# Two query heads in a pair of neighbouring PSUM banks, each half read by one pass of 1024 columns, with four banks for all other products

## The reference

```
x = x + tanh(g_xattn) * attention(layernorm(x), ctx, ctx, mask)     # 16 heads of 64
x = x + tanh(g_ffn)   * experts(layernorm(x))                       # 8 experts, top 2
attention: q = x Wq^T, k = ctx Wk^T, v = ctx Wv^T by heads
           softmax(q k^T + mask) v, then Wo
experts:   logits = x Wg + bg; p = softmax; the two largest, divided by their sum
           sum over the two of weight * (relu(x W1 + b1) W2 + b2)
```

## Time and profile before

| | |
|---|---|
| runs | 1152.84, 1154.45, 1154.65 us; median 1154.45 |
| the profiled execution | 1155.27 us, span 1153.5 |
| busy in the span | PE 881.5 us, DVE 939.9, ACT 785.6, POOL 710.6 |
| mean granted TensorE clock | 0.921 |

### The profile page before, as it was taken

The page is one execution under the profiler, slowest core; times in us unless marked ns, Lnnn a source line. Parts: engine busy times, 40 slices in busy tenths (PEclk is TensorE's granted clock), DMA queues, the critical chain, the costliest instruction groups (busy, mean ns, idle before and its releaser), DMA issues.

```text
span 1153.5 us, 33826 instructions
## 1 busy us (share of the span) xinstructions
PE 881.5 (76%) x11840; PEld 674.7 (58%) x11840; DVE 939.9 (81%) x2160; ACT 785.6 (68%) x1627; POOL 710.6 (62%) x701
## 2 busy tenths in 40 slices
PE   6787888798788888877897887878898767555560
PEld 4465665566566766666675656666676556444440
DVE  3888898898989897978888989978798987646633
ACT  3877778777677878786887667766887564444540
POOL 3143455547365666564658787755758787778775
PEclk9998899999999999999999998999998897778975
DMA  8367756555467765453445455554445465477773
GB/s 173 75 172 196 206 146 171 153 159 157 130 172 197 207 179 158 107 131 96 116 116 147 121 161 131 128 129 103 109 122 160 119 172 154 145 202 211 209 205 103
DMA packets 250791, 174.53 MB, mean 151 GB/s; under 512 B 39168, under 2 KB 232192, under 8 KB 250624
## 3 DMA queue, kind: packets, MB, share of 16 engines
q1 hardware_dynamic: 242432, 155.57, 50.9%
q0 software_dynamic: 8192, 16.79, 4.9%
HBM read 75.42 MB, written 63.84 MB: 121 GB/s over the span
## 4 chain that ended last, share of the span: by engine, by line
DVE 24%; issue 13%; PE 13%; POOL 8%; ACT 8%; SPq 3%; DMA 2%; DVEq 0%; POOLq 0%; ACTq 0%
PE bank L90 4%; POOL arena L1033 4%; PE bank L92 3%; PE bank L91 3%; DVE qL L726 3%; POOL hidL L1072 2%; DVE vL L901 2%; DVE row_max L929 2%; DVE otL L955 2%; DVE arena L909 2%; DVE x_back L949 2%; POOL slots L1020 2%; DVE row_sum L917 1%; SPq L1153 1%; ACT qH L545 1%
## 5 line engine op out<-in xcount | busy, mean ns | idle before, releaser
L1078 POOL TENSOR_TENSOR ptL<-pt,ptH 128x512 f16<-128x512 f32 x128 | 148.8, 1162 | 250.9 <-ACT pt L651 250.6
L726 DVE TENSOR_TENSOR qL<-bank,qH 128x512 f16<-128x512 f32 x256 | 173.7, 681 | 51.7 <-ACT qH L545 49.5
L545 ACT ACTIVATE qH<-bank 128x512 f16<-128x512 f32 x256 | 152.9, 599 | 43.8 <-PE bank L92 42.6
L1084 POOL TENSOR_TENSOR prob<-prob,row_inv 128x512 f32<-128x512 f32 x128 | 134.9, 1054 | 52.4 <-DVE row_inv L935 52.3
L1020 POOL DMA_INDIRECT slots<-x2hat,slot x128 | 128.1, 1001 | 31.9 <-issue 29.9
L90 PE MATMUL bank<-ptH,vdH 128*128 128x64 f16 x1024 | 120.4, 202 | 33.6 <-DVE arena L909 23.6
L1033 POOL DMA_INDIRECT arena<-slots,slot x128 | 123.1, 962 | 36.1 <-issue 29.7
L90 PE MATMUL bank<-arena,hidH 128*128 128x128 f16 x396 | 83.6, 240 | 69.6 <-POOL hidL L1072 66.9
L90 PEld LDWEIGHTS bank<-ptH,vdH 128*128 128x128 f16 x1024 | 107.9, 118 | 41.2 <-DVE arena L909 27.6
L1072 POOL TENSOR_TENSOR hidL<-arena,hidH 128x512 f16<-128x512 f32 x99 | 115.7, 1169 | 12.2 <-ACT hidH L595 10.8
L91 PE MATMUL bank<-ptL,vdH 128*128 128x64 f16 x1024 | 120.4, 202 | 0.0
(11 more groups left out here) (158 smaller groups left out, 3399.5 us busy)
## 6 DMA issues: line engine op xcount, KB each, us to landing
arena<-expert_weights SPq DMA_DIRECT2D x99, 321.0 KB, 3.1
slots<-zeros SPq DMA_DIRECT2D x60, 512.0 KB, 3.4
vdH<-vH SPq DMA_DIRECT2D x256, 64.0 KB
vdL<-vL SPq DMA_DIRECT2D x256, 64.0 KB
arena<-slots SPq DMA_DIRECT2D x99, 128.0 KB
slots<-arena SPq DMA_DIRECT2D x99, 128.0 KB
x_raw<-in_x SPq DMA_DIRECT2D x16, 256.0 KB, 4.1
ctx_raw<-in_ctx SPq DMA_DIRECT2D x16, 256.0 KB, 4.6
```

Of the source, the lines that this page charges most:

```text
L545: act.activation(qH[:, g % 2, 2 * j + g2, :, h2, :], bk("Q", g, h)[:, :].rearrange("p (b q) -> p b q", b=GB), ACT.Copy).then_inc(s_q_high, 1)
L726: dve.tensor_tensor(qL[at], bk("Q", g, h)[:, :].rearrange("p (b q) -> p b q", b=GB), qH[at], ALU.subtract).then_inc(s_q_low[h % 2], 1)
L1078: pool.tensor_tensor(ptL[:, b % 2, :], pt[:, b % 2, :], ptH[:, b % 2, :], ALU.subtract).then_inc(s_pt_low, 1)
L1084: pool.tensor_tensor(p, p, row_inv[:, b % NPB, :].unsqueeze(2).to_broadcast([P, JG, S]), ALU.mult).then_inc(s_normal, 1)
```

## The change

The two heads of a step now go into one tensor `head_pair` of two neighbouring banks. PE makes both heads' products one after the other at the start of the step and signals once; ACT copies both in one instruction of 1024 columns, and DVE reads both in one. Before PE writes the next pair it waits for DVE's read of the last. The remaining four banks rotate over all other products, so their owners follow each other in another order. On PE, `route` and `positions` move from the middle of the step to behind the experts' output.

```diff
-        bank = [stack.enter_context(nc.psum_tensor(f"bank{i}", [P, N], F32)) for i in range(NBANK)]
+        bank = [stack.enter_context(nc.psum_tensor(f"bank{i}", [P, N], F32)) for i in range(NBANK - 2)]
+        head_pair = stack.enter_context(nc.psum_tensor("head_pair", [P, 2, N], F32))
...
         def evicted(name):
             kind, *at = name
-            if kind == "Q":
-                g, h = at
-                return [(s_q_high, g * H + h + 1), q_lowered(g, h)]
...
-            def queries(g, h):
-                for freed in take_bank("Q", g, h):
-                    pe.wait_ge(*freed)
-                if h == 0:
+            def queries(g, i):
+                at = g * JG + i
+                if at:
+                    pe.wait_ge(s_q_low, at)
+                if i == 0:
                     pe.wait_ge(s_xT_low, g + 1)
-                if g == 0 and h % 4 == 0:
-                    pe.wait_ge(s_wdve, h // 4 + 1)
-                three_passes(pe, bk("Q", g, h)[:, :], (aH[:, h, :], aL[:, h, :]),
-                             (xtH[:, g % 2, :], xtL[:, g % 2, :])).then_inc(s_q, 1)
+                if g == 0 and i % 2 == 0:
+                    pe.wait_ge(s_wdve, i // 2 + 1)
+                for g2 in range(2):
+                    last = three_passes(pe, head_pair[:, g2, :], (aH[:, 2 * i + g2, :], aL[:, 2 * i + g2, :]),
+                                        (xtH[:, g % 2, :], xtL[:, g % 2, :]))
+                last.then_inc(s_q, 1)
...
                 if i == 0:
-                    pe.wait_ge(*q_lowered(g, H - 2))
-                    pe.wait_ge(*q_lowered(g, H - 1))
+                    pe.wait_ge(s_q_low, JG * (g + 1))
...
                 if within(g + 1, GROUPS):
-                    queries(g + 1, 2 * i)
+                    queries(g + 1, i)
                 if within(s // 2, TILES):
                     values(s // 2, s % 2)
-                if within(g + 1, GROUPS):
-                    queries(g + 1, 2 * i + 1)
-                if i == 0 and within(g - 2, GROUPS):
-                    route(g - 2)
...
-                if i == 2 and within(g - 2, GROUPS):
-                    positions(g - 2)
...
                 if unit_at(s - 2) is not None:
                     expert_out(unit_at(s - 2))
+                if i == 0 and within(g - 2, GROUPS):
+                    route(g - 2)
+                if i == 2 and within(g - 2, GROUPS):
+                    positions(g - 2)
...
-                j, h2, g2 = h // 4, h % 4 // 2, h % 2
-                act.activation(qH[:, g % 2, 2 * j + g2, :, h2, :], bk("Q", g, h)[:, :].rearrange("p (b q) -> p b q", b=GB),
-                               ACT.Copy).then_inc(s_q_high, 1)
+                j, h2 = i // 2, i % 2
+                act.activation(qH[:, g % 2, 2 * j:2 * j + 2, :, h2, :],
+                               head_pair[:, :, :].rearrange("p a (b q) -> p a b q", b=GB), ACT.Copy).then_inc(s_q_high, 1)
...
-                if within(g + 1, GROUPS):
-                    queries_high(g + 1, 2 * i + 1)
...
-                at = (slice(None), g % 2, 2 * j + g2, slice(None), h2, slice(None))
-                dve.tensor_tensor(qL[at], bk("Q", g, h)[:, :].rearrange("p (b q) -> p b q", b=GB), qH[at],
-                                  ALU.subtract).then_inc(s_q_low[h % 2], 1)
+                at = (slice(None), g % 2, slice(2 * j, 2 * j + 2), slice(None), h2, slice(None))
+                dve.tensor_tensor(qL[at], head_pair[:, :, :].rearrange("p a (b q) -> p a b q", b=GB), qH[at],
+                                  ALU.subtract).then_inc(s_q_low, 1)
...
-                if within(g + 1, GROUPS):
-                    queries_low(g + 1, 2 * i + 1)
```

More of the change, by code:

```diff
@@ L243, in flamingo_block @@
         s_xT_low, s_ctxT_low, s_x2T_low = sem("xT_low"), sem("ctxT_low"), sem("x2T_low")
-        s_q_low = [sem(f"q_low{i}") for i in range(2)]
-        s_v_low, s_max, s_shift, s_sum, s_inv, s_o_low, s_res = (
-            sem(n) for n in ("v_low", "max", "shift", "sum", "inverse", "o_low", "residual"))
+        s_q_low, s_v_low, s_max, s_shift, s_sum, s_inv, s_o_low, s_res = (
+            sem(n) for n in ("q_low", "v_low", "max", "shift", "sum", "inverse", "o_low", "residual"))
         s_marked, s_mask_in = sem("score_banks_marked"), sem("mask_in_bank")
@@ L263, in flamingo_block @@
             sem(n) for n in ("pt_low", "normal", "rank_before", "rank_add", "hid_low"))
-        def q_lowered(g, h):
-            return s_q_low[h % 2], g * (H // 2) + h // 2 + 1
         def x_loaded(g):
@@ L537, in _, with queries_high @@
         def _(act):
-            def queries_high(g, h):
-                act.wait_ge(s_q, g * H + h + 1)
-                if h == 0 and g >= 2:
+            def queries_high(g, i):
+                act.wait_ge(s_q, g * JG + i + 1)
+                if i == 0 and g >= 2:
                     act.wait_ge(s_scores, GB * (g - 1))
-                if h == 0 and g == 0:
+                if i == 0 and g == 0:
                     act.wait_ge(s_wdve, H // 4 + 5)
-                j, h2, g2 = h // 4, h % 4 // 2, h % 2
-                act.activation(qH[:, g % 2, 2 * j + g2, :, h2, :], bk("Q", g, h)[:, :].rearrange("p (b q) -> p b q", b=GB),
-                               ACT.Copy).then_inc(s_q_high, 1)
+                j, h2 = i // 2, i % 2
+                act.activation(qH[:, g % 2, 2 * j:2 * j + 2, :, h2, :],
+                               head_pair[:, :, :].rearrange("p a (b q) -> p a b q", b=GB), ACT.Copy).then_inc(s_q_high, 1)
             def transposed_high(name, g, high, after, freed, count):
@@ L624, in _ @@
                 if within(g + 1, GROUPS):
-                    queries_high(g + 1, 2 * i)
+                    queries_high(g + 1, i)
                 if within(s // 2, TILES):
@@ L666, in _ @@
                 if i == 6 and within(g + 2, GROUPS):
-                    transposed_high("xT", g + 2, xtH[:, g % 2, :], s_xT, (s_q, H * (g + 1)) if g >= 0 else None, s_xT_high)
+                    transposed_high("xT", g + 2, xtH[:, g % 2, :], s_xT, (s_q, JG * (g + 1)) if g >= 0 else None, s_xT_high)
                 if i == 6 - sooner and within(g + 1, GROUPS):
@@ L720, in ln_shift, with queries_low @@
                                          ALU.mult).then_inc(s_ln[w]["shift"], 1)
-            def queries_low(g, h):
-                dve.wait_ge(s_q_high, g * H + h + 1)
-                j, h2, g2 = h // 4, h % 4 // 2, h % 2
-                at = (slice(None), g % 2, 2 * j + g2, slice(None), h2, slice(None))
-                dve.tensor_tensor(qL[at], bk("Q", g, h)[:, :].rearrange("p (b q) -> p b q", b=GB), qH[at],
-                                  ALU.subtract).then_inc(s_q_low[h % 2], 1)
+            def queries_low(g, i):
+                dve.wait_ge(s_q_high, g * JG + i + 1)
+                j, h2 = i // 2, i % 2
+                at = (slice(None), g % 2, slice(2 * j, 2 * j + 2), slice(None), h2, slice(None))
+                dve.tensor_tensor(qL[at], head_pair[:, :, :].rearrange("p a (b q) -> p a b q", b=GB), qH[at],
+                                  ALU.subtract).then_inc(s_q_low, 1)
             def transposed_low(name, g, low, high, after, count):
@@ L896, in _ @@
                 if within(g + 1, GROUPS):
-                    queries_low(g + 1, 2 * i)
+                    queries_low(g + 1, i)
                 if within(s // 2, TILES):
```

## The result

| | before | after |
|---|---|---|
| median of 4 runs each | 1153.68 us | 1236.51 us (1235.24 to 1246.74) |
| ratio | | 1.0737, 95% interval 1.0679 to 1.0795 |
| span of the profiled execution | 1153.5 us | 1234.7 us |
| mean granted TensorE clock | 0.921 | 0.910 |

The table counts one run of the kernel before more than the one ahead of the prediction. The change makes the kernel slower by some 83 us (81 between the two spans). The direction, which was given 0.83, is right; 1188 and the range up to 1210 are too low.

What follows compares the result with a forecast made beforehand. DVE was taken as nearest to a bound where the change acts, though often starved waiting for ACT or PE. Groups without experts +9, with experts +23, start and end +1 gave +33 us on 1155.3: 1188 us, range 1160 to 1210.

Steps and rivals of the forecast that it cites:

- The instruction of 1024 columns: Query reads: a pair takes 1214 ns on DVE and 1030 on ACT, saving 0.06 us per saturated step, at most 8 us.
- A group without experts, +1.5: Eight-step groups in steps 6 to 48: later DVE query starts cost 1.5 us each, six groups, +9 us.
- The mechanism with experts: Groups with experts: the pair delays DVE's read of the experts' output, PE waits for its bank, making the next queries late.
- The loop through L909: DVE reads the experts' output, PE gets the bank, makes the next queries, ACT and DVE read them, then L909 again.
- A group with experts, 2.6: Nine groups, steps 54 to 119: 2.6 us lost in each, +23 us; bounds 1.3 and 5 a group.
- the 3.8 worked out: Steps 70 to 73, plus the step with i = 4: a group with experts loses some 3.8 us.
- the cut to two thirds: Groups with experts: 3.8 us taken as 2.6, since gathers holding up DVE and POOL cover part of the loss.
- The start, counted as part of +1: First queries run straight through all three engines; start and end together cost +1 us.
- The wait for the pair's banks, costed at nothing: PE's new wait for DVE's read of the last pair: nothing, since DVE is done before PE wants the pair.
- The rival of the banks: PE's delays for the pair's banks in saturated steps add 20 to 37 us: 1210 to 1225, chance 0.07.
- The end, in the same +1: From step 120, without queries, banks wanted up to 0.5 us early until 130, then POOL sets the pace; +1 with the start.
- What to look at, as the prediction set it: Expected signs: DVE idle before queries 75 us or more, DVE busy down about 20, expert groups 2 to 4 longer, end unchanged.

Runs made afterwards that it cites:

- e2: Kernel before, with 512-column reads in their old places, but two banks for the heads, four for the rest, route and positions late: 1166.2 us, ratio 1.0109.
- e6: Changed kernel with the pair moved to the old second head's place, behind the values on PE and the row sum on DVE: 1183.99 us, ratio 1.0262.
- e8: Changed kernel with DVE's read of the experts' output moved to the head of its step, ahead of the queries: 1182.44 us, ratio 1.0224.
- e4: Changed kernel, but pairs take two neighbouring banks of one ring of six for all products; route and positions in old places: 1213.3 us, ratio 1.0505.
- e3: Changed kernel with each pair read as two 512-column instructions on ACT and DVE and a signal per head: 1184.04 us, ratio 1.0261.
- e5: Changed kernel with PE signalling each head and ACT reading 512 columns twice; DVE still reads 1024: 1217.72 us, ratio 1.0563.
- e9: Kernel before with pairs only in steps i = 2 to 5 from group 1, one ring of six: 1176.74 us, ratio 1.0042, on another chip.
- e1: Changed kernel, but group 0 (steps -8 to -1) signals and reads queries head by head, each with its own bank: 1225.25 us, ratio 1.0622.
- e7: Kernel before with DVE's read of the experts' output moved to the head of its step, ahead of the queries: 1137.18 us, ratio 0.9845.

## Why the prediction was right in kind and wrong in size

- *The instruction of 1024 columns: right*, to 5 ns on DVE and 9 on ACT. In groups without experts each saturated step came out 0.06 us shorter.
- *A group without experts, +1.5: the links right, the sum too large.* Measured after step 45: 0.43, 0.90, 1.84 and 1.73 us late in steps 46 to 49 (predicted 0.43, 0.95, 1.6 and about 1.75). Most groups then win back some 0.5 in the steps behind, so a group of eight costs 0.8 to 1.2, and steps 8 to 15 are 3.3 shorter than before. That is why steps 0 to 47 cost some 1.6 us in all, where 9 was forecast. The 3.3 are not the pair's doing: e2, without a pair, is 4.9 shorter there, and in step 8 DVE had stood idle for 3.76 us in front of the values and now does for 1.61.
- *The mechanism with experts: right.* The loop through L909 and the waits of DVE for ACT and of PE for that read lie where they were put; e6 and e8 shorten it and win most of the middle's loss back, and e2 and e4 rule out the number of banks as its cause.
- *A group with experts, 2.6: wrong, and this term and the start's are the steps that failed.* Steps 40 to 111 cost 47.0 and steps 112 to 118 another 4.8, where 1.5 and nine groups of 2.6 were forecast, 25 in all. The nine stretches of eight steps from 40 cost 0.8, 2.8, 4.7, 9.4, 5.6, 6.0, 3.1, 7.4 and 7.2. Two things were left out of the 3.8 worked out: PE's lower clock behind longer waits (0.43 a pass for 0.22), and the steps with i = 3, which lost 3.6 us (67 to 68) and 2.1 (75 to 76). The third error is the cut to two thirds. It took stretches in which gathers hold up DVE and POOL as cover. In a closed loop idle time of DVE is none, since the engine that idles is a link of the loop itself; this is argued, no run tests it. That the clock adds to the loss is read from the passes. How many us of the 47 it makes was not taken apart, but PE's busy time in steps 40 to 111 rises from 451.2 to 462.0 us for the same work (granted clock 0.96 and 0.94), so an estimate of its share is at most 11 us.
- *The start, counted as part of +1: wrong, measured +25.* "The first queries run straight through all three engines" was the term that should have been priced. With a single pair buffer the term is PE's six passes + ACT's read + DVE's read for each of eight steps, 1.3 + 1.0 + 1.2 and the hand-overs, 3.84 us as the first step shows (29.08 to 32.92 on DVE), where before took 15.1 / 8 = 1.9. That makes 16 us that could have been worked out from the rows at hand. The fall of the clock adds the rest: six steps of 5.12 instead of 3.84 and one of 4.19 are another 8, and 24 were measured.
- *The wait for the pair's banks, costed at nothing: wrong at the start, covered or absent later.* The rows that I looked at (333.52, 340.27 in the earlier trace rows) lie at steps where PE is late, and I took them for all. Of PE's 30.6 us of waiting for the pair, 17.3 lie at steps -7 to 0; the rest lies at steps 2 to 44, in a group without experts 1.07, 0.84 and some 0.55 us at i = 2, 3 and 5; from step 45 on there is none. The rival of the banks, given 0.07 with 1210 to 1225, placed this wait in saturated steps. It is there, but PE's lead covers it: the steps with i = 2 and 3 came out 0.06 us shorter.
- *The end, in the same +1: measured +3.6 behind step 119,* from the four banks or the late `route` (e2 +4.6, e3 +2.4, e4 with six and the old place +0.3).
- *What to look at, as the prediction set it:* DVE's idle time up from 51.7 to 75 or more held (126.5). DVE's busy time fell by 10.2 us, 17.6 of it less in the queries, with other rows longer; 20 had been expected. Two signs did not come: the groups with experts cost 2.8 to 9.4 us, not 2 to 4, and the last 150 us are some 3 us longer, not unchanged.

The sum put right, start 25.0, steps 0 to 118 52.6 (0.8 + 47.0 + 4.8), end 3.6, makes the 81 us between the spans.

The Trainium skill, Perfetto Trace Analysis, section Optimizing Scalar/DVE Operations, says both that larger operations pay if the engine is saturated and that, where ACT or DVE are not saturated but leave bubbles on other engines, breaking instructions up may finish the work sooner. By the second, this change goes the wrong way, and the runs agree: two reads instead of one on ACT give 19 us (e5), on both engines with single signals 52 (e3). By the first, pairing should pay where DVE is full; in e9 the full steps with i = 2 and 3 are 0.06 us shorter, but the kernel is at +0.4%. The Trainium skill's section Matmuls on the same page asks for independent groups to rotate through banks so that reads overlap the next products; the start agrees, with 38.7 us for one buffer of two banks, 21.4 for the same two banks taken singly (e1) and 19.2 for pairs in a ring of six (e4).

## What to carry to other kernels

Joining two reads saves the fixed part of one instruction (0.06 us here) and makes everything that hangs on the first half wait for the second, once on each engine of the chain; count that chain before the saving. Where a stream has its own buffer, work out one turn alone (make, read, read, release) and set it against the time between turns, above all at the start, where nothing else covers it. And look for the short read that gives back a bank others wait for: put ahead of the long ones (e7) it won 1.55% by itself.

## What the hardware showed that was not expected

- A slow chain can slow TensorE too: with PE idle for 1.5 to 2.4 us in each step, the granted clock over 35 us was 0.57 and passes of 512 columns came 0.43 us apart, which made a step 5.12 us instead of 3.84; broken into single heads, the same work had 1.00 (e1).
- Two neighbouring banks in one instruction cost nothing extra: 1219 ns on DVE and 1021 on ACT, within 10 ns of the line through 256 and 512 columns within one bank.
